# Scans that begin with the constant 0, four tiles' states folded in, and low-rank products between halves of the modulation blocks

## The reference

```python
mod = (_silu(L0_c) @ L0_wmod).reshape(L0_c.shape[0], 6, 1, -1)
sa, ca, ga, sb, cb, gb = (mod[:, 0], mod[:, 1], mod[:, 2], mod[:, 3], mod[:, 4], mod[:, 5])
h = _layernorm(x, axis=-1) * (1 + ca) + sa
x = x + ga * _L0_attn_ref(h, ...)
h = _layernorm(x, axis=-1) * (1 + cb) + sb
...
out = einsum('bsd,hd->bsh', x, w) + einsum('bsr,hr->bsh', einsum('bsd,rd->bsr', x, a), b)   # gate, up, down
...
def step(state, inp):                       # layer 1, N = 16 states for each of 1024 channels
    dt_t, B_t, C_t, u_t = inp
    dA = jnp.exp(dt_t[..., None] * A)
    state = state * dA + (dt_t * u_t)[..., None] * B_t[:, None, :]
    y = jnp.einsum('bdn,bn->bd', state, C_t)
    return (state, y)
```

## Time and profile before

| | us |
|---|---|
| median of 3 runs | 1528.91 |
| lowest, highest | 1527.16, 1529.26 |
| profiled execution | 1526.18 |
| its span | 1524.0 |
| busy: TensorE | 1358.3 |
| busy: VectorE | 1241.0 |
| busy: GpSimd | 1026.9 |
| busy: ScalarE | 945.7 |

### The profile page before, as it was taken

The page is one execution under the profiler, slowest core; times in us unless marked ns, Lnnn a source line. Parts: engine busy times, 40 slices in busy tenths (PEclk is TensorE's granted clock), DMA queues, the critical chain, the costliest instruction groups (busy, mean ns, idle before and its releaser), DMA issues.

```text
span 1524.0 us, 25264 instructions
## 1 busy us (share of the span) xinstructions
PE 1358.3 (89%) x8817; PEld 1005.7 (66%) x8817; DVE 1241.0 (81%) x1644; ACT 945.7 (62%) x2585; POOL 1026.9 (67%) x697
## 2 busy tenths in 40 slices
PE   7789999999999959689899899899889989988777
PEld 5467677768776648568568667667767766855543
DVE  5684664456443479999999999999999999999994
ACT  3332343233321577788888788788788888886751
POOL 0343243213212397898998999899899899899870
PEclk9699999999999979999999999999999999999579
DMA  9432222101100200100110110020020020020001
GB/s 336 166 105 62 83 84 84 56 29 36 36 28 16 77 25 1 56 29 15 57 42 1 57 56 1 31 81 1 15 98 1 15 88 11 1 71 28 0 1 42
DMA packets 32388, 77.16 MB, mean 51 GB/s; under 512 B 3667, under 2 KB 4723, under 8 KB 31750
## 3 DMA queue, kind: packets, MB, share of 16 engines
q1 hardware_dynamic: 32262, 75.55, 14.5%
HBM read 66.99 MB, written 8.55 MB: 50 GB/s over the span
## 4 chain that ended last, share of the span: by engine, by line
PE 33%; DVE 13%; POOL 12%; issue 6%; ACT 4%; DVEq 0%; ACTq 0%; POOLq 0%
PE ps_h L1490 11%; DVE h L2261 8%; POOL h L2120 5%; POOL dbu L2085 5%; PE ps_m L1454 4%; DVE acc L2277 3%; PE ps_o L1514 2%; PE ps_m L165 2%; PE ps_m L166 2%; PE ps_m L167 2%; PE ps_s L1454 2%; ACT ps_a L1745 2%; PE ps_m L1414 1%; ACT ab L1877 1%; PE ps_s L165 1%
## 5 line engine op out<-in xcount | busy, mean ns | idle before, releaser
L2261 DVE TENSOR_TENSOR_SCAN h<-ps_a,carry,dbu 128x512 f32<-128x512 f32 x512 | 626.8, 1268 | 14.7 <-ACT ps_a L1745 5.0
L2085 POOL TENSOR_TENSOR dbu<-dtu,b_all 128x1020 f32<-128x1020 f32 x256 | 598.6, 2362 | 20.9 <-DVE h L2261 20.9
L1745 ACT ACTIVATE ps_a<-dt,a_neg 128x256 f32<-128x256 f32 (+1 forms) x1024 | 442.6, 465 | 80.1 <-DVE h L2261 79.7
L1490 PE MATMUL ps_h<-ident,h 128*128 128x128 f32 x1536 | 227.5, 291 | 72.9 <-DVE acc L2277 64.0
L2277 DVE SCALAR_TENSOR_TENSOR acc<-ps_h,c_cur,acc 128x512 f32<-128x512 f32 x384 | 268.2, 739 | 9.1 <-PE ps_h L1490 8.6
L1490 PEld LDWEIGHTS ps_h<-ident,h 128*128 128x128 f32 x1536 | 183.8, 149 | 132.5 <-DVE h L2261 101.7
L713 POOL TENSOR_TENSOR hid_l<-hid,hid_h 128x256 f16<-128x256 f32 (+1 forms) x88 | 77.7, 885 | 156.1 <-ACT hid_h L605 156.1
L2120 POOL TENSOR_TENSOR h<-h,c_all 128x1024 f32<-128x1024 f32 x64 | 151.3, 2365 | 16.3 <-ACT carry L1765 16.3
L597 ACT ACTIVATE sil<-ps_gu 128x256 f32<-128x256 f32 (+1 forms) x88 | 33.9, 385 | 179.4 <-PE ps_gu L167 179.4
L165 PE MATMUL ps_m<-h_h,wi_h 128*128 128x256 f16 x432 | 120.0, 278 | 2.7 <-PEq L155 2.4
L166 PE MATMUL ps_m<-h_l,wi_h 128*128 128x256 f16 x432 | 119.8, 277 | 0.0
(11 more groups left out here) (404 smaller groups left out, 2871.8 us busy)
## 6 DMA issues: line engine op xcount, KB each, us to landing
b_all<-bt_scratch SPq DMA_DIRECT2D x32, 512.0 KB, 3.7
wm<-in_wmod SPq DMA_DIRECT2D x7, 1024.0 KB, 5.1
wo<-in_wmod SPq DMA_DIRECT2D x5, 1024.0 KB, 6.9
xa<-in_x SPq DMA_DIRECT2D x8, 512.0 KB, 4.4
stage<-in_W_in SPq DMA_DIRECT2D x4, 1024.0 KB
x_scratch<-x SPq DMA_DIRECT2D x8, 512.0 KB, 3.1
c_all<-bt_scratch SPq DMA_DIRECT2D x8, 512.0 KB, 6.1
x<-x_scratch SPq DMA_DIRECT2D x8, 512.0 KB, 3.6
```

The lines of the kernel that those rows point to most:

```text
L1490: tr = pe.transpose(ps_h[:, t, j * P:(j + 1) * P], h[:, s % RING, j, t * P:(t + 1) * P], W["ident"][:])
L1745: ex = nc.scalar.activation(ps_a[:, j, j % 2:], dt[:, m, j % 2:], ACT.Exp, scale=a_neg[:, m, st:st + 1])
L2085: nc.gpsimd.tensor_tensor(dbu[:, s % AHEAD, :, 1:], dtu[:, :, 1:], b_all[:, st, 1:].unsqueeze(1).to_broadcast([P, DG, CH - 1]), ALU.mult). ...
L2261: nc.vector.tensor_tensor_scan(h[:, s % RING, two].rearrange("p j t -> p (j t)"), ps_a[:, two].rearrange("p j t -> p (j t)"), dbu[:, s % A ...
```

## The change

Three things. In layer 1 the scans begin with the constant 0 instead of a column of carry, and the fold covers all four tiles: decay0 is twice as large, first_decay makes four exponentials, old_state and first_inputs work on four tiles. In the begin of layer 0, modulation 4 writes to other columns of its bank than 3, so that it no longer waits for VectorE to read 3, and blocks 3 and 4 are made in halves, with the products of G3, U0 and U1 ahead of, between and after the halves; U2's stands before `turn(1)`, U3's behind it. VectorE's and ScalarE's lists are put in an order to match: G2's add moves ahead of the first gate's steps, G3's behind them, U0's and U1's around the statistics of the second norm, and both scale and shift are read after the whole of 4.

```diff
-    mod_at = (mod_bank, ps_o[:, 1], turn_bank[1], mod_bank, mod_bank, turn_bank[0])
+    mod_at = (mod_bank, ps_o[:, 1], turn_bank[1], mod_bank, mod_bank[:, KD:], turn_bank[0])
...
-        def modulation(i):
+        def modulation(i, part=range(KD)):
...
-            elif i in (3, 4):
-                pe.wait_ge(S["mod_done"], i)
...
-                for q in range(KD):
+                for q in part:
...
+                if KD - 1 not in part:
+                    return
             mm.then_inc(S["wmod_used"], 1)
...
         linear(0, True)
-        modulation(3)
         lora(G3)
-        modulation(4)
+        modulation(3, range(0, 2))
+        lora(U0)
+        modulation(3, range(2, KD))
+        modulation(4, range(0, 2))
+        lora(U0 + 1)
+        modulation(4, range(2, KD))
+        lora(U0 + 2)
         turn(1)
-        for n in range(U0, NP):
-            lora(n)
+        lora(U0 + 3)
         modulation(5)
...
         for n in range(G0, U0):
             high_part(n)
+        for n in range(U0, U0 + 2):
+            high_part(n)
         act.wait_ge(S["mod_done"], 5)
         high(1, 1, h2_h)
-        for n in range(U0, NP):
+        for n in range(U0 + 2, NP):
             high_part(n)
...
-            dve.wait_ge(S["wmod_used"], i + 1)
+            dve.wait_ge(S["wmod_used"], 5 if i == 3 else i + 1)
...
         low_part(G1)
+        add_lora(G2)
         adaln_0(2)
+        add_lora(G3)
...
         add_linear(0, True)
+        add_lora(U0)
         statistics(1, x1)
-        add_lora(G2)
+        add_lora(U0 + 1)
         normalise(1, x1)
         adaln_0(3)
-        add_lora(G3)
         adaln_0(4)
-        add_lora(U0)
-        add_lora(U0 + 1)
         add_lora(U0 + 2)
-        low(1, h2_h, h2_l, hT)
         add_lora(U0 + 3)
         low_part(U0 + 2)
+        low(1, h2_h, h2_l, hT)
         low_part(U0 + 3)
...
-    decay0 = sb("decay0", [P, KI // 2, NS], F32, c)
+    decay0 = sb("decay0", [P, KI, NS], F32, c)
...
-            for m in (g * DG + 1, g * DG + 3):
-                op = nc.scalar.activation(decay0[:, m // 2, :], a_neg[:, m, :], ACT.Exp, scale=dt[:, m, 0:1])
+            for m in range(g * DG, (g + 1) * DG):
+                op = nc.scalar.activation(decay0[:, m, :], a_neg[:, m, :], ACT.Exp, scale=dt[:, m, 0:1])
...
-            old = decay0[:, g * 2:g * 2 + 2, :]
-            nc.gpsimd.tensor_tensor(old, old, carry[:, steps, :].rearrange("p n (a b) -> p b a n", b=2)[:, 1], ALU.mult)\
+            old = decay0[:, g * DG:(g + 1) * DG, :]
+            nc.gpsimd.tensor_tensor(old, old, carry[:, steps, :].rearrange("p n j -> p j n"), ALU.mult)\
...
-            odd = fold[:, steps, :].rearrange("p n (a b) -> p b n a", b=2)[:, 1]
-            nc.gpsimd.tensor_tensor(odd, odd, decay0[:, g * 2:g * 2 + 2, :].rearrange("p a n -> p n a"), ALU.add)\
+            nc.gpsimd.tensor_tensor(fold[:, steps, :], fold[:, steps, :], decay0[:, g * DG:(g + 1) * DG, :].rearrange("p j n -> p n j"), ALU.add)\
...
-                                             carry[:, s, 2 * half:2 * half + 1], ALU.mult, ALU.add).then_inc(S["scan_half"], 1)
+                                             0.0, ALU.mult, ALU.add).then_inc(S["scan_half"], 1)
```

## The result

The change makes the kernel faster. Median of 4 runs: **1513.46 us** (1511.24 to 1515.37) against 1528.99 (1527.16 to 1529.26); ratio 0.990, 95% interval 0.9882 to 0.9919, so about 15.5 us less. A second comparison on another occasion gave 1515.51 against 1529.14, ratio 0.9911 (0.9898 to 0.9925). The profiled execution took 1514.93 us. The forecast was 1517.1, between 1503 and 1525.

What follows compares the result with a forecast made beforehand. No single engine bounds layer 1: VectorE is full beside TensorE, then beside GpSimd; the begin's end moves everything. Layer 1's 6.6 us (of 31 gross) plus the begin's 5.2 make 11.8, giving a median of 1517.1 us, range 1503 to 1525.

Steps and rivals of the forecast that it cites:

- The scan: Layer 1's 512 scans: a constant first value saves 0.06 us each, 31 us of VectorE gross; mean about 1205 ns.
- Rival B: Layer 1's scans: the constant costs what the read cost, no shortening; 1524.5 us, between 1522 and 1527; chance 0.16.
- Stretch A: Layer 1, step 16 to 23 of a chunk: GpSimd's time alone, so shorter scans give nothing and VectorE merely waits.
- Stretch B: Layer 1, step 23 to 6 of the next chunk: GpSimd unbroken; gain 0.3 before dt and 0.1 at the end.
- Stretch C: Layer 1, step 7 to 16, TensorE full: nine steps' scans win 0.07, steps 7 and 16 0.12 each; gain 0.3.
- The folds: Layer 1, two GpSimd operations widened to 128x64, 0.05 us each: first group's on GpSimd's path, 0.1 per chunk; second's covered.
- Rival D: Layer 1: first group's folds, reading carry turned round, cost as much as a wide operation (2.34 us); 1545.1 us; chance 0.07.
- First and last chunk: Layer 1's end chunks, lacking one side of the pipeline: 1.5 us gain each, between 0.6 and 3.8.
- The begin: Begin of layer 0: first gate/up matmul at 71.5 instead of 76.74, set by modulation 5's weights; 5.2 us, bounds 3 to 7.
- Rival A: Layer 1: all of the scans' 31 us reaches the end, plus 5.2; 1492.7 us; chance 0.08.
- Rival C: Begin: TensorE keeps its full clock, modulation halves win 4.8 us more; 1512.3 us; chance 0.14.
- signs named: Layer 1: some 20 us more VectorE idle, ended by ps_h (steps 6, 22), dbu (23), ps_a (16); GpSimd, TensorE busy times unchanged.

Runs made afterwards that it cites:

- zero_column: The kernel after, with the scans' first value read from a 128x1 column of zeros in SBUF instead of the constant 0; 1524.86 us against 1529.11 for before, ratio 0.9969.
- The two extra kernels: The kernel after with four more GpSimd products ahead of the first group's fold (1535.42 us, ratio 1.0036) or the second group's (1515.48 us, ratio 0.9909).
- light_after: The kernel after with a quarter of GpSimd's two wide products left out from the second chunk on; 1500.04 us, ratio 0.9805.
- no_overlap: mod5_early with GpSimd's first low part beside U0's add, its copy of x behind VectorE's low parts, h's low part before both u_l; 1511.37 us, ratio 0.9883.
- mod5_early: After, with GpSimd's low parts held until the second normalise, that ahead of U1's add, and modulation 5's weights requested before the wait for modulation 4; 1517.26 us, ratio 0.9909.
- extra_group0: The kernel after with four more GpSimd products (128x64, carry read turned round) ahead of the first group's fold, in seven turns; 1535.42 us, ratio 1.0036.

## Why the prediction was right, point by point

The number was right, 1517.1 for 1513.5, and so was the likeliest case: the scan's gain came and most of it was lost to the engines beside it. In the begin the number came by luck, as said below. Of the 3.6 us of difference 3.2 lie in layer 1 (9.8 for 6.6) and 0.5 in the begin (5.7 for 5.2).

- **The scan, 0.06 us each, 31 gross.** Right: 1209 ns for about 1205, 1.12 from start to start for 1.125, and zero_column names the operand as the cause. Rival B is out. The Trainium skill, "VectorE: DVE Perf Modes", section Scalar operands, names no difference between a constant and a per-partition operand; the trace has 0.06 us.
- **Stretch A, nothing.** The number is right (23.28 to 23.31), the reason half right: GpSimd does bound it, but "VectorE merely waits" is wrong; with GpSimd lighter and the scans as before it won only 0.2 us (23.09). The 0.12 put down for step 16 (in C) didn't come. Its second half's carry waits in ScalarE's list behind h_l, and h_l for TensorE, 0.28 both before and after; GpSimd's first h starts 2.91 after the scan of step 16, as it did (2.90).
- **Stretch B, 0.3 net.** It gave 0.49. GpSimd's 0.28 in front of dt went, as forecast (before has 7 such waits, after 2). Mis-sized is the end, put at 0.1: from the end of GpSimd's fourth h to acc it took 2.61 us (917.53 to 920.14) and takes 2.27 (912.04 to 914.31). The step that I missed is ScalarE's copy of the sum. In before it started at 918.62, since it stood in its list behind a carry that waited for VectorE's scan; now it starts at 912.84, on TensorE's signal:

```profile
917.71 0.21 ACT L1765 ACTIVATE carry<-h 128x4 f32<-128x4 f32 x1 [0.36 <-DVE h L2261]
917.83 0.86 ACT L1745 ACTIVATE ps_a<-dt,a_neg 128x256 f32<-128x256 f32 x2
918.62 1.06 ACT L1937 ACTIVATE acc<-ps_h 128x512 f32<-128x512 f32 x2
```

```profile
912.84 1.08 ACT L1943 ACTIVATE acc<-ps_h 128x512 f32<-128x512 f32 x2 [1.11 <-PE ps_h L1481]
```

- **Stretch C, 0.07 and 0.12 for step 7.** 0.24 measured for 0.19, at the size of what is argued; no run takes it apart.
- **The folds.** 0.1 forecast, 0 to 0.2 measured. Rival D (they cost as much as wide products) is out: 352 and 349 ns. The two extra kernels show that the first group's does lie on the path and the second's doesn't.
- **First and last chunk, 1.5 each.** Mis-sized: 2.8 and 1.9. In the first chunk TensorE has no output of a chunk before to make, and the steps from 7 to 16 fall from 37.80 to 36.25, more than the 1.10 that nine shorter steps can give. The other kernels with the long scan have 36.88 to 37.00 there and a first chunk of 124.0 to 125.2, so part of the 2.8 is the draw of one execution. The bounds, 0.6 to 3.8, held; taking the lower end because "A and B are the same" was the error.
- **The begin, 5.2, to 71.5 by modulation 5.** 5.7 measured, but by other hands. In before's time (after less 1.94) modulation 5 starts at 64.6 for the 65.3 of the forecast and ends at 70.2; the last low part ends at 71.0 for 70.0, and TensorE starts at 71.07. Two errors of about 1 us each crossed, one down and one up; that 5.7 lies so near 5.2 is luck. The step that failed is "costs nothing, cover 1 us" for the late normalise: it was stretched by 3.0, ended 2.7 later than put down, and made turn(1) wait 1.85. What the prediction left out is that GpSimd's earlier low parts run beside it.
- **Rival A** (all 31 pay out): out, and light_after shows what it would have needed. **Rival C** (full clock in the begin): out. TensorE's granted clock in after, by stretch (length, busy us, clock), is 0.50 (1.2 GHz) from 48 to 70 us, behind a wait of 1.51 for G3's add:

```profile
42.00:46.00 4.00, 3.43 (x25) 1.00 0.89 369
46.00:48.00 2.00, 1.06 (x3) 0.61 0.00 0
48.00:58.00 10.00, 10.00 (x47) 0.50 0.00 1
58.00:70.00 12.00, 9.02 (x24) 0.50 0.81 255
```

- **Rival E** (no change): out, by 12 us at the least.
- Of the signs named, VectorE's further idle time in layer 1 is 18 us (40.4 for 22.3 between the first scan and the last) where some 20 were named. Two of the four places are right in the fourth chunk: ps_h at step 6 (0.27 and 1.04) and dbu at step 23 (0.52). None stands at step 22, ps_a ends a wait at step 19 (0.24) and not at 16, and the wait for carry at step 2, not named, grew from 0.39 to 0.51. TensorE's busy time fell by 5.7 us where none was named.

## What to carry to other kernels

When two engines are both full, making one lighter pays little until the other is made lighter too. In layer 1 GpSimd's lighter products alone gave 2.4 us (986.7 to 984.3), the shorter scans alone 9.8, and both together 22.9. A cheap probe is to leave out some of the other engine's work in both versions. The scans' per-partition value had a price (0.06 us an instruction here), so fold it into an operand that another, idle place can prepare. A reordering that lets GpSimd start earlier must be read against VectorE's operations in the same stretch that take all their inputs from SBUF, for in the cases below the two took turns.

## What the hardware showed beyond this

- VectorE's normalise, h_l and u_l, all on SBUF alone, and GpSimd's work took turns: a normalise of 0.54 us lasted 3.007 beside a 2.97 us low part; GpSimd's copy of 1.04 us lasted 2.40 beside two of VectorE's. It shows as busy time and not as a wait. Not held were the adds with one operand in PSUM (1.58 or 1.59 in all), nor, in no_overlap, the statistics with their one input in SBUF (1.28 beside a low part of 2.80).
- A wait of 2.90 us of TensorE was followed by a granted clock of 0.50 (1.2 GHz), and 1.74 us of delay a chunk grew to 2.45; a wait of 2.81 in another chunk was not followed by slow matmuls.
- With its weights early, modulation 5 took 3.67 us (mod5_early, no_overlap) at a granted clock of 1.00; in after it took 5.60, and the clock was 0.50 up to 70 us. TensorE had waited for about 1 us ahead of it in all three (0.90 to 1.22); what set the clock free earlier isn't shown.
- What comes before w_l moves everything by up to 4.2 us (w_l at 33.02 to 37.23 in these profiles): gains of a few us in the begin are read from distances, not from spans.
- What stays open: why the unchanged part between gate and up and the first scan varies from 456 to 463 us over these kernels; and how the clock and the rest share extra_group0's excess: from step 7 to 16 its fourth and fifth chunks also take 0.9 and 1.4 us more.
